# The opening of the first attention: context in tiles of 256 KB, loads held on the queue, the second value projection behind two queries

## The reference

```python
q = rope(layernorm(x) @ wq)     # 32 heads of 128
k = rope(ctx @ wk)              # 8 key heads of 128, each shared by 4 query heads
v = ctx @ wv
x = x + tanh(g) * (softmax(q @ k.T / sqrt(128) + mask) @ v) @ wo
```

## Time and profile before

| what | us |
|---|---|
| median of 3 runs | 867.3 (865.81 to 867.38) |
| the profiled execution, its own time | 866.32 |
| its span, first to last instruction | 864.5 |
| PE busy in the span | 827.7 |
| mean granted TensorE clock | 0.984 |

### The profile page before, as it was taken

One profiled execution on the slowest core, in us unless ns is written; L12 is line 12 of the kernel. 1 busy time (PEld: TensorE's weight loads), 2 busy tenths in 40 slices (PEclk: granted clock), 3 DMA queues, 4 the chain that ended last, 5 costly groups with the idle time before them and its releaser, 6 DMA issues. The chain is left out here.

```text
span 864.5 us, 13698 instructions
## 1 busy us (share of the span) xinstructions
PE 827.7 (96%) x5021; PEld 652.5 (75%) x5021; DVE 570.0 (66%) x1095; ACT 440.5 (51%) x832; POOL 474.3 (55%) x410
## 2 busy tenths in 40 slices
PE   5889999999999999999999999998889999999996
PEld 5668888888888888888888888886536776777774
DVE  2867666565665566555565455546799999998862
ACT  3555455554554444444445534331378766677640
POOL 1567645665566664566456665352237664656550
PEclk9999999999999999999999999999889999999997
DMA  9420322322323223131130121065233232331100
GB/s 269 123 86 25 110 86 60 109 82 51 110 57 85 66 66 93 38 110 58 39 117 25 41 26 1 1 230 136 55 89 83 51 86 55 75 74 44 44 13 25
DMA packets 73155, 64.73 MB, mean 75 GB/s; under 512 B 35793, under 2 KB 53425, under 8 KB 72705
## 3 DMA queue, kind: packets, MB, share of 16 engines
q1 hardware_dynamic: 71600, 63.26, 27.1%
q10 hardware_dynamic: 1488, 0.59, 0.3%
HBM read 47.01 MB, written 6.34 MB: 62 GB/s over the span
## 5 line engine op out<-in xcount | busy, mean ns | idle before, releaser
L770 DVE SCALAR_TENSOR_TENSOR x_res<-bank,gate,x_res 128x512 f32<-128x512 f32 x128 | 95.7, 748 | 96.7 <-PE bank L469 95.7
L934 POOL TENSOR_TENSOR prob<-prob,row_inv 128x512 f32<-128x512 f32 x32 | 33.4, 1044 | 192.7 <-DVE row_inv L766 192.6
L920 POOL TENSOR_TENSOR rope_swap<-rope_swap,trig 128x512 f32<-128x512 f32 x80 | 104.1, 1302 | 33.0 <-ACT rope_swap L589 33.0
L741 DVE TENSOR_TENSOR rope_cos<-bank,trig 128x512 f32<-128x512 f32 x80 | 54.7, 684 | 76.8 <-PE bank L80 76.8
L78 PE MATMUL bank<-xnT_hi,wq_hi 128*128 128x512 f32 x256 | 103.8, 405 | 1.4 <-DVE xnT_lo L705 1.4
L464 PE MATMUL bank<-wo_hi,oT_hi 128*128 128x512 f32 x256 | 101.8, 398 | 2.6 <-issue 1.2
L465 PE MATMUL bank<-wo_lo,oT_hi 128*128 128x512 f32 x256 | 101.8, 398 | 0.0
L80 PE MATMUL bank<-xnT_hi,wq_lo 128*128 128x512 f32 x256 | 101.6, 397 | 0.0
L79 PE MATMUL bank<-xnT_lo,wq_hi 128*128 128x512 f32 x256 | 101.2, 395 | 0.0
L588 ACT COPY rope_swap<-bank 64x512 f32<-64x512 f32 x80 | 46.7, 584 | 89.6 <-DVE rope_cos L741 89.0
L926 POOL TENSOR_TENSOR q_rope<-rope_cos,rope_swap 128x512 f32<-128x512 f32 x64 | 83.2, 1301 | 5.0
(11 more groups left out here) (225 smaller groups left out, 1951.6 us busy)
## 6 DMA issues: line engine op xcount, KB each, us to landing
wq_raw<-in_L_xattn_wq SPq DMA_DIRECT2D x16, 512.0 KB, 4.0
wo_raw<-in_L_xattn_wo SPq DMA_DIRECT2D x16, 512.0 KB, 3.9
xn<-in_L_ffn_Wd SPq DMA_DIRECT2D x16, 256.0 KB, 3.0
b_k_twice<-b_qk_hi SPq DMA_DIRECT2D x32, 128.0 KB, 2.4
w_T_dram<-w_out SPq DMA_DIRECT2D x28, 128.0 KB, 2.4
w_T<-w_T_dram SPq DMA_DIRECT2D x2, 1376.0 KB, 7.3
xn<-in_L_ffn_Wg SPq DMA_DIRECT2D x10, 256.0 KB, 4.0
xn<-in_L_ffn_Wu SPq DMA_DIRECT2D x10, 256.0 KB, 2.9
```

The source lines that it names most:

```text
L741: dve.tensor_tensor(out=rope_cos[:, rp, :].rearrange("p (b s) -> p b s", s=S), in0=proj[pos % 2][:, :].rearrange("p (b s) -> p b s", s=S), ...
L770: dve.scalar_tensor_tensor(out=K.x[:, t, :], in0=wo_ps[t % 2][:, :], scalar=K.gate[:, 0:1], in1=K.x[:, t, :], op0=ALU.mult, op1=ALU.add).t ...
L920: pool.tensor_tensor(out=sw, in0=sw, in1=sin_b, op=ALU.mult).then_inc(s_rope, 1)
```

## The change

- **Context loads.** Eight loads of one tile (256 KB), each with a semaphore of its own; PE waits tile by tile.
- **Held loads.** SP issues context tiles 0 to 2, and from there on each further load only when an earlier one has landed, up to the mask. The first value weights move from ACT's queue to SP's, behind x load 0.
- **Order of items.** `("v", 1)` goes from place 3 to place 5 and is computed in two parts, one before tiles 12 to 14 and one before tile 15. Items 3 (now q 0 0) and 6 (q 0 1) are computed in two parts of 256 columns, each as soon as its two tiles of x are split. The value transposes of half 1 go behind item 6.
- **DVE's order.** `bn(0)` to `bn(3)` and `times_cos(0, 0)` go between the lo tiles of the context, and the lo part of the first key weights is done on DVE instead of POOL, behind `lo_tile(0)`.
- **ACT's order.** `v_copy(0, 0)` goes behind the tiles 8 to 11 and `evacuate(0, 2)`; the later steps follow the new order of items.

```diff
-        FIRST = [("k", 0), ("v", 0), ("k", 1), ("v", 1), ("q", 0, 0), ("q", 1, 0), ("q", 0, 1), ("q", 1, 1),
+        FIRST = [("k", 0), ("v", 0), ("k", 1), ("q", 0, 0), ("q", 1, 0), ("v", 1), ("q", 0, 1), ("q", 1, 1),
...
@@ sync
-            for i in range(4):
-                load_ctx(i)
-            for i in range(3):
-                load_x(i)
+            for t in range(3):
+                load_ctx(t)
+            sp.wait_ge(s_ctx_in[0], 16)
+            load_ctx(3)
+            sp.wait_ge(s_ctx_in[1], 16)
+            load_x(0)
+            sp.wait_ge(s_ctx_in[2], 16)
+            load_wkv(0, 1)
+            sp.wait_ge(s_ctx_in[3], 16)
+            load_ctx(4)
+            load_ctx(5)
+            sp.wait_ge(s_x_in[0], 16)
+            load_x(1)
+            sp.wait_ge(s_wkv_in[1], 16)
+            load_ctx(6)
+            sp.wait_ge(s_ctx_in[4], 16)
+            load_ctx(7)
+            sp.wait_ge(s_ctx_in[5], 16)
+            load_x(2)
+            sp.wait_ge(s_x_in[1], 16)
             load_wq(0, 0)
+            sp.wait_ge(s_ctx_in[7], 16)
             load_x(3)
+            sp.wait_ge(s_x_in[2], 16)
...
@@ tensor, behind tiles 8 to 11
-            item(0, 3)
-            pe.wait_ge(s_tr_lo, NT + UT)
+            for part in range(2):
+                pe.wait_ge(s_tr_lo, NT + 2 * part + 2)
+                item(0, 3, part)
             item(0, 4)
+            item(0, 5, 0)
+            for n in range(NT + UT, 2 * NT - 1):
+                transpose_tile(n)
+            item(0, 5, 1)
+            transpose_tile(2 * NT - 1)
+            for part in range(2):
+                pe.wait_ge(s_tr_lo, NT + UT + 2 * part + 2)
+                item(0, 6, part)
             pe.wait_ge(s_v, 1)
             v_transpose(0, 1, trans)
-            item(0, 5)
-            for n in range(NT + UT, 2 * NT):
-                transpose_tile(n)
-            pe.wait_ge(s_tr_lo, 2 * NT)
-            item(0, 6)
             item(0, 7)
@@ scalar
-            load(wkv_raw[1][:, :, :], wv_dram.rearrange("(c p) n -> p c n", p=P)[:, :, 0:DH], s_wkv_in[1])
...
-            v_copy(0, 0, trans)
             for n in range(NT, NT + UT):
                 hi_tile(n)
             evacuate(0, 2)
+            v_copy(0, 0, trans)
             evacuate(0, 3)
+            hi_tile(NT + UT)
+            hi_tile(NT + UT + 1)
+            evacuate(0, 4)
+            hi_tile(NT + UT + 2)
+            evacuate(0, 5)
+            hi_tile(NT + UT + 3)
             for c in range(NQP):
                 wq_piece(1, 0, c)
-            evacuate(0, 4)
+            evacuate(0, 6)
             v_copy(0, 1, trans)
-            for n in range(NT + UT, 2 * NT):
-                hi_tile(n)
-            evacuate(0, 5)
             for c in range(NQP):
                 wo_piece(0, 0, c)
-            evacuate(0, 6)
@@ vector
-            for n in range(NT):
+            lo_tile(0)
+            split(wkv_raw[0][:, :, :], wkv_hi[0][:, :, :], wkv_lo[0][:, :, :], s_wkv_hi, s_wkv_lo, 1)
+            for n in range(1, UT):
                 lo_tile(n)
+            bn(0)
+            bn(1)
+            lo_tile(UT)
+            lo_tile(UT + 1)
+            bn(2)
+            bn(3)
             dve.wait_ge(s_trig_in, 16)
             times_cos(0, 0)
-            for t in range(UT):
-                bn(t)
+            lo_tile(UT + 2)
+            lo_tile(UT + 3)
             aggregate(range(0, UT), 2 * UT)
...
-            times_cos(0, 4)
+            times_cos(0, 3)
             for t in range(UT, UT + 3):
                 normalise_tile(t)
-            times_cos(0, 5)
+            times_cos(0, 4)
@@ gpsimd
-            for which in range(2):
-                wkv_piece(0, which)
+            pool.wait_ge(s_wkv_lo, 1)
+            wkv_piece(0, 1)
...
-            for pos in (4, 5, 6, 7):
+            for pos in (3, 4, 6, 7):
                 rotate(0, pos)
```

More of the change, by code:

```diff
@@ L141, in attention_block @@
         sem = cx.sem
-        s_ctx_in = [sem(f"s_ctx_in{i}") for i in range(4)]
+        s_ctx_in = [sem(f"s_ctx_in{i}") for i in range(NT)]
         s_x_in = [sem(f"s_x_in{i}") for i in range(4)]
@@ L280, in load_wkv, with load_ctx @@
                 sp.dma_start(wkv_raw[which][:, :, :], src).then_inc(s_wkv_in[which], 16)
-            def load_ctx(i):
-                sp.dma_start(ctx_nat[i // 2][:, 2 * (i % 2):2 * (i % 2) + 2, :], ctx_v[:, 2 * i:2 * i + 2, :]
-                             ).then_inc(s_ctx_in[i], 16)
+            def load_ctx(t):
+                sp.dma_start(ctx_nat[t // 4][:, t % 4, :], ctx_v[:, t, :]).then_inc(s_ctx_in[t], 16)
             def load_x(i):
                 sp.dma_start(K.x[:, 2 * i:2 * i + 2, :], x_v[:, 2 * i:2 * i + 2, :]).then_inc(s_x_in[i], 16)
-            for i in range(4):
-                load_ctx(i)
-            for i in range(3):
-                load_x(i)
+            for t in range(3):
[18 more added lines that the diff above has]
+            sp.wait_ge(s_x_in[1], 16)
             load_wq(0, 0)
+            sp.wait_ge(s_ctx_in[7], 16)
             load_x(3)
+            sp.wait_ge(s_x_in[2], 16)
             for h in range(2):
@@ L392, in transpose_tile @@
                 if n < NT:
-                    pe.wait_ge(s_ctx_in[t // 2], 16)
+                    pe.wait_ge(s_ctx_in[t], 16)
                     src = ctx_nat[t // 4][:, t % 4, :]
@@ L714, in aggregate @@
             def aggregate(tiles, done):
-                for k, t in enumerate(tiles):
-                    dve.wait_ge(s_stat, t + 1 + (UT + 1 if t >= UT + 2 else 0))
+                for t in tiles:
+                    dve.wait_ge(s_stat, t + 1 + (UT if t >= UT else 0))
                     dve.bn_aggr(meanvar[:, t, :], stats[:, t, :]).then_inc(s_stat, 1)
@@ L771, in accumulate @@
                                          in1=K.x[:, t, :], op0=ALU.mult, op1=ALU.add).then_inc(s_acc, 1)
-            for n in range(NT):
+            lo_tile(0)
+            split(wkv_raw[0][:, :, :], wkv_hi[0][:, :, :], wkv_lo[0][:, :, :], s_wkv_hi, s_wkv_lo, 1)
+            for n in range(1, UT):
                 lo_tile(n)
+            bn(0)
[4 more added lines that the diff above has]
+            bn(3)
             dve.wait_ge(s_trig_in, 16)
             times_cos(0, 0)
-            for t in range(UT):
-                bn(t)
+            lo_tile(UT + 2)
+            lo_tile(UT + 3)
             aggregate(range(0, UT), 2 * UT)
-            for t in range(UT, UT + 2):
-                bn(t)
+            bn(UT)
+            bn(UT + 1)
             for t in range(3):
@@ L787, in _ @@
                 lo_tile(NT + t)
-            for t in range(UT + 2, NT):
-                bn(t)
+            bn(UT + 2)
+            bn(UT + 3)
             aggregate(range(UT, NT), 2 * NT)
-            times_cos(0, 4)
+            times_cos(0, 3)
             for t in range(UT, UT + 3):
                 normalise_tile(t)
-            times_cos(0, 5)
+            times_cos(0, 4)
             lo_tile(NT + UT)
```

## The result

The changed kernel takes 861.7 us (median of 5 runs, 860.57 to 863.02), the kernel before 867.3 (5 runs, 865.62 to 868.66). The profiled execution took 861.39 us, with a span of 859.6, against 866.32 and 864.5. Timed again later beside the kernel before (third group of the experiments), the changed kernel took 7.8 us less: ratio 0.9914 (0.989 to 0.9939).

A forecast was written before the change was run, and what follows sets the result against it. DVE's chain bounds the opening up to 32.5 us, PE behind it; 866.32 - 2.8 - 1.1 = 862.4 us profiled, with the median 1.0 above it 863.4, range 861 to 866.4 (8 in 10).

The forecast's parts named there:

- Sum: Whole kernel: -2.8 and -1.1 give 862.4 us profiled; the median, 1.0 above it, 863.4; forecast's chance 0.52.
- rival D: Whole kernel: more gain than forecast, -4.9 to 862.4 us, with no contention and weights early; chance 0.05.
- The first loads: Start of item 0: smaller context loads gain nothing, the split on DVE costs a little; PE starts at 8.45, +0.15 us.
- The held loads: SP's queue in the opening: nobody waits for the held loads, 4 us and more of cover each; priced at nothing.
- Rival B: Opening loads: held loads become a chain of round trips and the kernel slower, such as 866.7 or 871; chance 0.10.
- From the context to x: Lo 7 to the fourth tile of x: statistics and times_cos leave DVE's chain, normalise starts at 23.9, -2.8 us.
- A fall in item 2 itself would be free, as DVE's chain hides it: PE's item 2 after its idle time: a clock fall there would cost nothing.
- From x to the scores: Fourth tile of x to first scores: 17.1 of work and 1.3 of waits against 19.52 us, -1.1.
- price of 0.6: Second normalise group: without contention from POOL the stretch to the scores would be 0.6 us shorter.
- Behind the scores: After the first scores: softmax and slots follow as before, so all shifts alike.
- Rival C: Behind the scores: the gain is given back, as wq, wo and softmax or clock falls set PE; 866.5 to 867.3, chance 0.13.
- Rival A: Second half of the opening gives nothing, through POOL contention (+0.9) or a clock fall (up to 1.4); 864.5 us, chance 0.20.

The follow-up runs named there:

- third group of the experiments: Later runs beside the kernel before (median 870.26 us): POOL's split of wq 0 or both normalise groups' POOL work held, and the changed kernel again, 862.45 us, 0.9914.
- DVE's order alone: Kernel before with only bn 0 to 3 and times_cos(0, 0) moved between the lo tiles on DVE; 865.04 us, ratio 0.997.
- rotation held: Changed kernel with POOL waiting before the rotation of item 3 until tiles 4 to 6 of x are normalised; 860.46 us, ratio 0.9925.
- two in flight: Changed kernel with each opening load issued when the one two places before has landed, never more than two in flight; 860.71 us, ratio 0.9928.
- the experiment that held the split of wq 0: Changed kernel with POOL waiting before the two lo parts of wq 0 until tiles 0 to 2 of x are normalised; 862.23 us, 0.9912.
- The order alone: Kernel before with only the new order of items, and PE's, ACT's, POOL's and DVE's steps that follow it; 866.91 us, ratio 0.9983.
- the split moved: Changed kernel with the split of wo 0 (hi on ACT, lo on DVE) behind the first softmax instead of ahead; 865.0 us, ratio 0.9969.
- the kernel before with the split held: Kernel before with POOL waiting ahead of the lo parts of wq 0 until three tiles of x are normalised; 865.29 us, ratio 0.9955.

## Why the prediction was right

**Sum.** Predicted -2.8 and -1.1 on the profiled execution, measured -3.2 and -0.94. To the scores: 4.14 against 3.9. The rest of the measured 4.9 was no term of mine: -1.15 in the tail, less the 0.4 given back before it. The forecast of 863.4 also took the median to lie 1.0 above the profiled execution; it lay 0.3 above. The measured 861.7 is in fact nearer to rival D's 862.4, which had a chance of 0.05, than to the forecast; of D's two reasons the early weights came true and the missing contention did not. And beside the second timing of the changed kernel (7.8 us less, 5.3 to 9.6) the sum of 3.9 explains only half. So the mechanism up to the scores is right, and that the total fell inside the range is partly luck. The range itself doesn't follow from the bounds given for it: added up on each side of 863.4 they give 861.6 to 867.0, not 861 to 866.4. The tail's length in the twelve executions of the experiments went from 264.8 to 267.8 us. The longest, of DVE's order alone, had the clock of the kernel before in the two windows above (0.83 and 0.83); rotation held had 0.97 and 0.95, and 265.5 us. So a slow clock there goes with a long tail, but it is not all: two in flight had the same clock in both windows as rotation held, and 266.4 us. Why the clock falls less there in some executions, what else sets the length, and whether the opening has a part in it stays open.

**The first loads (+0.15).** Measured -0.06 in this execution and about -0.5 in the means of all executions: the sign was wrong. Tile 0 at 4.30 (predicted 4.0), tile 1 at 5.73 (4.95). "They land no earlier" was wrong: the key weights were cast from 5.00, not 5.39. Item 0 then waited for tile 1 and its hi and lo, not for the weights. With the split on POOL it was 0.08 later, which is within the spread of the nine executions (0.46), with the old loads 0.59 later, which is outside it.

**The held loads (nothing).** Right in effect. PE waited for no DMA behind the second tile, and with the old loads the time was the same. Rival B is out: with only two in flight, tile 7 cost 0.82 us. The Trainium skill, DMA: Bandwidth & Descriptors (Rules for kernel authors), asks for 1 MiB or more per DMA where the most bandwidth is wanted; no run here shows what following it would bring, as nobody waited for these loads. The covers were thinner than forecast. SP issues each held load when the one it waits for has landed, so its timeline dates the landings: the value weights at 10.6 (predicted 9.5, cast at 13.12), context 7 at 16.1 (14.1, turned behind 19.2), x 2 at 17.8 (15.6, its statistics at 22.1). That leaves 2.5 us for the value weights and 3 to 4.5 for the others.

**From the context to x (-2.8).** Right, and shown by itself: DVE's order alone gave 2.8 in its one profile (32.50 to 29.69). The 0.4 more of the changed kernel lie ahead of lo 7: item 1 started at 16.34 instead of 16.66, mostly because the turning of context tiles 2 and 3 took 1.63 us against 1.91. In the second execution it took 1.91 again, and the fourth tile came at 30.72, 1.8 us and not 3.2 ahead of the kernel before. Group at 23.44 (predicted 23.9), 4.38 long (4.3); item 2 at 22.30 (22.65) after 2.07 idle (1.95). "A fall in item 2 itself would be free, as DVE's chain hides it" was nearly right: the clock did fall, and the transposes of vT that follow it began at 26.7, with the fourth tile waiting 0.68 us for DVE. But the experiment that held the split of wq 0 shows that the cover was almost used up: half a us.

**From x to the scores (-1.1).** Right in size in the first profile: 18.58 us against 18.4, but as the sum of two errors, work of 17.64 (predicted 17.1) and waits of 0.94 (1.3). In the second profile and five more with this order it was 19.0 us, a gain of 0.5, half of the forecast. The first query's wait was 0.54 (0.75), lo 15's 0.15 (0.2). The second group did meet POOL: 3.40 us (about 3.35). The Trainium skill's sentence on the shared interfaces (GPSIMD Engine Reference, Key points) agrees with the groups of 1.46 and 3.40 us, though no row says in which port mode DVE ran. Its price of 0.6 was 0.1 in the first profile, where POOL paid for the first tile and PE had other work for the rest, and 0.55 in the others. The order alone gave 0.5 in its one profile and 0.9983 in its runs, which doesn't settle its size by itself.

**Behind the scores ("all shifts alike").** Right to 0.2 us, but by another way. A new wait of 1.52 us for `prob` stands at 56.95, because DVE splits wo 0 until 50.3, does the softmax after it, and its subtraction at 52.29 takes 1.77 us beside a busy POOL, where the other softmax steps take 0.7; the wait of 1.24 for `probT` of the kernel before is gone instead. Rival C had the place right and the size wrong. With the split moved, a good part of the gain was given back there (0.9969), though not all of it, as C had it.

**Rival A.** Its clock fall is real (DVE's order alone lost some 1.5 us to one), and did not strike the changed kernel at a place that counts. Its row, a fall after 3.4 us of idle time, is no rule: in the kernel before with the split held, item 2 kept the higher clock after the same 3.41 us. Of the 5.6 us, DVE's order carries about half (0.997; 0.6 to 4.6 us by its interval), which was the part with the clearest row.

No kernel here beat the changed one by more than its interval; rotation held (0.9925) and two in flight (0.9928) are the lowest of their group, and the changed kernel itself had 0.994 and 0.9914.

## What to carry to other kernels

A wait without a named releaser is worth following to the other engines' rows before any edit: here PE's longest wait behind the first load was hidden by another chain (in the kernel before with the split held it stayed at 3.41 us and the fourth tile came 3.0 us earlier), and work of DVE that could have been done while it idled set the end. When two chains end within a fraction of a us, an edit to one of them buys only that fraction, so the same line (a held split on POOL) is worth some 4 us in one version (0.9955, with an interval from 1.7 to 6) and nothing in the next. Run the same kernel twice before a landmark is read to better than 2 us.

## What the runs showed of the hardware that I had not expected

- The two mask loads took SP's queue 10.05 us to issue with nine loads issued on that queue in the 5 us before, and 1.46 us at 17.78 when the loads before them had been held.
- An fp32 `normalise_tile` of 128x512 took 0.49 us beside an idle POOL and 1.46 beside a busy one, three times in a row in the first group (4.38 us). Which of the two engines pays changed with a few hundredths of a us: with DVE starting at 35.54 and POOL at 35.65, DVE's tile took 0.55 and POOL's rotation 1.59; in the second execution, with starts at 36.97 and 37.06, they took 1.67 and 1.30.
- PE's clock rose for the first time at different points in two executions of one kernel (a matmul of 256 columns at 14.02 took 0.39 and 0.58 us), and fell after 2.07 us of idle in one (0.55 over 22.30 to 23.50), and not after about 2.1 in another kernel's (1.00 over 21.90 to 24.70). Before the first rise the granted clock reads 1.00 all the same (over 8.50 to 10.70, where matmuls of 256 columns follow each other every 0.21 us instead of 0.12), so there only their pitch tells the level.
- The same 3.41 us of idle time ahead of item 2 were followed by a granted clock of 0.50 in the kernel before, and by full pitch in the kernel before with the split held (0.47 us for the matmul at 23.55).
